# A two-block transformer with graph routing on one core: 128-token groups in the convolution, fill tiles written by ScalarE, gathers placed ahead of loads

## The reference

```
x = x + L1_conv(ln_c(x))        # 3x3 convolution of quantized activations and weights
t = to_tokens(x)                # 50176 tokens of 128 channels
u = ln_t(t)
h = u @ W_gat                   # 4 heads x 4 experts = 16 numbers for each token
a_src, a_dst = (h*att_src).sum(-1), (h*att_dst).sum(-1)       # 4 + 4 numbers
for each destination node: softmax over its edges of leaky_relu(a_src[src] + a_dst[dst]),
    agg = sum of h[src] * alpha                               # 524288 edges and one self loop each
scores = mean over heads of layernorm(agg + b_gat); the top 2 of 4 experts get softmax weights
out = t + sum over experts of weight * (gelu(u @ W1 + b1) @ W2 + b2)
```

## Time and profile before

| | |
|---|---|
| Runs | 10778.33, 10784.39 (median), 10784.59 us |
| The profiled execution | 10787.32 us, span of its instructions 10785.5 us |
| Busy share of the span | POOL 57%, DVE 51%, PE 42%, ACT 36%, PEld 25% |
| Convolution, first to last scatter | 4175.6 to 4800.5 us |
| Graph, first to last gather | 4823.6 to 10024.8 us |
| Combination, first to last gather | 10065.6 to 10707.4 us |
| Granted TensorE clock, mean | 0.732 of full speed |

### The profile page before, as it was taken

One profiled execution on the slowest core, in us unless ns is written; L12 is line 12 of the kernel. 1 busy time (PEld: TensorE's weight loads), 2 busy tenths in 40 slices (PEclk: granted clock), 3 DMA queues, 4 the chain that ended last, 5 costly groups with the idle time before them and its releaser, 6 DMA issues. The chain is left out here.

```text
span 10785.5 us, 111540 instructions
## 1 busy us (share of the span) xinstructions
PE 4563.0 (42%) x31813; PEld 2715.7 (25%) x31813; DVE 5474.9 (51%) x14162; ACT 3929.5 (36%) x9657; POOL 6184.6 (57%) x6259
## 2 busy tenths in 40 slices
PE   0011777777758997873222222223223223223000
PEld 0011555555544444541111111111111101101000
DVE  9987999999986775541121121121121112112487
ACT  0011888888854554332121111112112112112255
POOL 0000555555532224667777777777777777777675
PEclk9755999999978998876666666666666666666555
DMA  0000111111121223543222222222222222222366
GB/s 20 2 0 34 40 39 38 39 41 38 39 78 55 62 62 100 141 121 55 44 46 49 44 46 49 44 42 53 44 42 53 44 42 53 44 42 48 134 250 244
DMA packets 1326096, 663.81 MB, mean 62 GB/s; under 512 B 1058255, under 2 KB 1239100, under 8 KB 1320764
## 3 DMA queue, kind: packets, MB, share of 16 engines
q1 hardware_dynamic: 1142396, 576.49, 19.5%
q0 software_dynamic: 183104, 80.22, 5.7%
HBM read 344.86 MB, written 313.71 MB: 61 GB/s over the span
## 5 line engine op out<-in xcount | busy, mean ns | idle before, releaser
L1832 POOL DMA_INDIRECT gr_rec<-rec,gr_idx x4096 | 3954.2, 965 | 1248.8 <-issue 1248.0
L1853 PE MATMUL gr_p_h<-gr_tT,gr_w 128*128 128x512 f32 x1568 | 849.4, 696 | 3671.7 <-ACT gr_hT L1887 3638.7
L1972 DVE TENSOR_SCALAR gr_pen<-gr_same 128x64 f32<-128x64 f32 x64 | 13.7, 213 | 3170.6 <-DMA gr_rec<-rec,gr_idx 3170.6
L1853 PEld LDWEIGHTS gr_p_h<-gr_tT,gr_w 128*128 128x128 f32 x1568 | 347.6, 227 | 4154.9 <-ACT gr_hT L1887 3723.8
L544 POOL TENSOR_TENSOR at_sq<-at_qk 128x256 f32<-128x256 f32 x392 | 290.2, 740 | 1844.1 <-ACT at_qk L594 1843.9
L1900 ACT ACTIVATE gr_ee<-gr_dd 128x512 f32<-128x512 f32 x64 | 40.3, 629 | 3588.0 <-DVE gr_dd L1991 3588.0
L1858 PE MATMUL gr_p_y<-gr_hT,gr_w 128*128 128x512 f32 x1568 | 688.9, 592 | 0.0
L1952 DVE STREAM_TRANSPOSE gr_z<-gr_yb 128x2048 f32<-128x2048 f32 x98 | 226.5, 2311 | 902.8 <-issue 491.5
L1887 ACT ACTIVATE gr_hT<-gr_p_h,gr_b 128x512 f32<-128x512 f32 x784 | 517.6, 688 | 191.7 <-PE gr_p_h L1853 191.0
L2140 POOL DMA_INDIRECT cb_a<-scan,cb_idx x392 | 499.0, 1273 | 133.7 <-issue 122.4
L1340 POOL DMA_INDIRECT adst<-co_rec,co_idx x448 | 424.5, 948 | 223.3 <-issue 123.1
(11 more groups left out here) (358 smaller groups left out, 13212.1 us busy)
## 6 DMA issues: line engine op xcount, KB each, us to landing
y<-gr_z SPq DMA_DIRECT2D x392, 256.0 KB, 5.4
cb_y<-y SPq DMA_DIRECT2D x28, 3584.0 KB, 13.2
gr_rec<-rec,gr_idx POOLq DMA_INDIRECT x4096, 2.3
scan<-gr_out SPq DMA_DIRECT2D x64, 768.0 KB, 3.8
at_xs<-in_x_win SPq DMA_DIRECT2D x56, 448.0 KB, 3.8
x<-at_x SPq DMA_DIRECT2D x56, 448.0 KB, 4.2
ff_x<-x SPq DMA_DIRECT2D x56, 448.0 KB, 3.4
x<-ff_x SPq DMA_DIRECT2D x784, 32.0 KB
```

The lines of the kernel that those rows point to most:

```text
L1832: nc.gpsimd.indirect_dma_start(out=rec[s][:, j, :], out_offset=None, in_=rec_dram, in_offset=bass.IndirectOffsetOnAxis(ap=idx[s][:, j:j + ...
L1853: nc.tensor.matmul(p_h[m % 4][:, :], w1[:, P * m:P * (m + 1)], tT[b.k][:, :], start=True, stop=True).then_inc(S["hp"], 1)
```

## The change

- Convolution: the tokens of a strip, 8 x 112 = 896, are taken as 7 groups of 128. The matmul for `rec` runs 7 times with 128 tokens, `rec` has 128 partitions x 7 groups, and there are 7 scatters of 128 indices a strip. Their indices are read from columns of `first` directly, so the tile `idx`, its copy on VectorE and its wait are gone. The x3 store has semaphores of its own (`x_out`) and stands ahead of the wait for `rec`; VectorE's x3 waits for that store alone. A strip's node order begins in the middle of a group, so `rec` is stored by four DMAs in place of two.
- Graph: SyncE's first DMA is the index load of chunk 0; GpSimd's first 64 gathers wait for it alone, and the `headr` gather comes after them. VectorE waits for `headr` at chunk 0.
- Combination: the index tile `end` has a semaphore of its own, and its columns are used directly. ScalarE fills both landing tiles at the start, and each later one behind the Exp that makes the inverse deviation (the tile's old content has been read by then).

```diff
-        rec = two("rec", [W, ROWS, REC])
+        rec = two("rec", [P, GROUPS, REC])                        # GROUPS = 7
...
@@ convolve, sync
                     if p.has(-1):
                         s = p.slot(-1)
+                        p.wait("x3", -1, 2)
+                        sp.sem_inc(S["passed"], 1)
+                        dst = x3_dram.rearrange("(y x) c -> x y c", x=W)[:, bass.ds((p.t - 1) * ROWS, ROWS), :]
+                        sp.dma_start(dst, x3[s][:, :, :]).then_inc(S[f"x_out{s}"], 16)
                         p.wait("rec", -1)
                         p.wait("tT", -1, 2)
...
-                        for h in range(2):
-                            dst = rec_dram.rearrange("(y x) c -> x y c", x=W)[:, bass.ds(token_row(nc, p.t - 1, h), HROWS), :]
-                            sp.dma_start(dst, rec[s][:, HROWS * h:HROWS * h + HROWS, :]).then_inc(S[f"out{s}"], 16)
+                        for row, q in ((top, 0), (low + P // 2, full + 1)):
+                            dst = rec_dram[row:row + full * P, :].rearrange("(g p) c -> p g c", p=P)
+                            sp.dma_start(dst, rec[s][:, q:q + full, :]).then_inc(S[f"out{s}"], 16)
+                        for row, lo in ((top + full * P, 0), (low, P // 2)):
+                            sp.dma_start(rec_dram[row:row + P // 2, :], rec[s][lo:lo + P // 2, full, :]).then_inc(S[f"out{s}"], 16)
@@ convolve, tensor
-                        for r in range(ROWS):
-                            mm = nc.tensor.matmul(p_r[:, r, :], tT[s][:, r, :], wcat[:, :], start=True, stop=True)
+                        for q in range(GROUPS):
+                            mm = nc.tensor.matmul(p_r[:, q, :], tokens[:, P * q:P * q + P], wcat[:, :], start=True, stop=True)
@@ convolve, gpsimd
-                        for r in range(ROWS):
-                            nc.gpsimd.indirect_dma_start(out=adst_dram, out_offset=bass.IndirectOffsetOnAxis(ap=idx[s][:, r:r + 1], axis=0),
-                                                         in_=rec[s][:, r, FEAT + GH:REC], in_offset=None, bounds_check=E - 1,
+                        for q in range(GROUPS):
+                            g = (p.t - 1) * GROUPS + q
+                            nc.gpsimd.indirect_dma_start(out=adst_dram, out_offset=bass.IndirectOffsetOnAxis(ap=first[:, g:g + 1], axis=0),
+                                                         in_=rec[s][:, q, FEAT + GH:REC], in_offset=None, bounds_check=E - 1,
@@ convolve, vector
-                        p.wait_lot("out", -2, CONV_OUT)
+                        p.wait_lot("x_out", -2, 16)
...
-                        p.wait_lot("sc", -2, ROWS * 16)
-                        nc.vector.tensor_copy(idx[s][:, :], first[:, bass.ds(p.t * ROWS, ROWS)]).then_inc(S["idx"], 1)
@@ graph_and_experts, sync
+                sp.dma_start(idx[0][:, :], src_dram.rearrange("(p e) -> p e", p=P)[:, 0:CH]).then_inc(S["ix0"], 16)
                 sp.wait_ge(S["set"], 1)
@@ combine, gpsimd
-                pool.wait_ge(S["consts_in"], 48)
-                pool.wait_ge(S["set"], 1)
+                pool.wait_ge(S["end_in"], 16)
...
-                        nc.gpsimd.tensor_copy(a[s][:, :, :], low[:, :, :])
-                        nc.gpsimd.tensor_copy(idx[s][:, :], end[:, bass.ds(p.t * FB, FB)]).then_inc(copied, 1)
-                        pool.wait_ge(copied, p.t + 1)
+                        p.wait("fill", 0)
@@ combine, scalar
+                for i in range(2):
+                    nc.scalar.activation(a[i][:, :, :], low[:, :, :], ACT.Copy).then_inc(S["fill"], 1)
...
                         nc.scalar.activation(rstd[:, :], lnv[:, :], ACT.Exp, scale=-0.5).then_inc(S["act"], 1)
+                        if p.has(3):
+                            nc.scalar.activation(a[p.slot(1)][:, :, :], low[:, :, :], ACT.Copy).then_inc(S["fill"], 1)
```

More of the change, by code:

```diff
@@ L1196 @@
 REC = FEAT + 2 * GH
+GROUPS = WIN * W // P
+FPARTS = 4
+FROWS = B * H * W // P // FPARTS
 def convolve(nc, d, pixels, x2_dram, x3_dram, tT_dram, rec_dram, recs_dram, start_dram, adst_dram):
@@ L1228, in convolve @@
         tT = two("tT", [P, ROWS, W])
-        rec = two("rec", [W, ROWS, REC])
+        rec = two("rec", [P, GROUPS, REC])
         p_c = [ps(f"p_c{i}", [P, HROWS, W]) for i in range(2)]
         p_t = [ps(f"p_t{i}", [P, HROWS, W]) for i in range(2)]
[L1232 to L1237, removed]
+        p_r = ps("p_r", [P, GROUPS, REC])
+        first_i = sb("first_i", [FROWS, FPARTS, P], I32)
+        first_f = sb("first_f", [FROWS, FPARTS, P])
+        first = sb("first", [P, FPARTS * FROWS], I32)
+        p_f = ps("p_f", [P, FPARTS, FROWS])
         p_x = [ps(f"p_x{i}", [W, HROWS, P]) for i in range(2)]
@@ L1240, in convolve @@
         own = {n: ctx.enter_context(nc.semaphore("co_" + n)) for n in (
-            "consts_in", "tanh", "ext", "top", "wq", "x_in0", "x_in1", "out0", "out1", "win", "conv", "xc", "px", "x3", "stat",
-            "rstd", "t", "trp", "tT", "recp", "rec", "first", "firstp", "idx", "passed")}
+            "consts_in", "tanh", "ext", "top", "wq", "x_in0", "x_in1", "x_out0", "x_out1", "out0", "out1", "win", "conv", "xc", "px", "x3", "stat",
+            "rstd", "t", "trp", "tT", "recp", "rec", "first", "firstp", "passed")}
         S = {**own, **dict(zip(("sc0", "sc1"), d["soft"][13:15]))}
@@ L1282, in _ @@
                 pe.wait_ge(S["first"], 1)
-                for b in range(B):
-                    mm = nc.tensor.transpose(p_f[:, b, :], first_f[:, b, :], ident[0:H, 0:H])
+                for b in range(FPARTS):
+                    mm = nc.tensor.transpose(p_f[:, b, :], first_f[:, b, :], ident[0:FROWS, 0:FROWS])
                 mm.then_inc(S["firstp"], 1)
@@ L1391, in _ @@
                 v.wait_ge(S["firstp"], 1)
-                nc.vector.tensor_copy(first[:, :], p_f[:, :, :].rearrange("x b y -> x (b y)")).then_inc(S["first"], 1)
+                nc.vector.tensor_copy(first[:, :], p_f[:, :, :].rearrange("p a g -> p (a g)")).then_inc(S["first"], 1)
                 for k in range(2):
@@ L2076, in combine @@
         S = {n: ctx.enter_context(nc.semaphore("cb_" + n)) for n in (
-            "consts_in", "set", "in0", "in1", "xy0", "xy1", "pre", "f", "sq", "act", "sum", "prod", "out0", "out1", "passed", "passed_sp")}
+            "end_in", "fill", "consts_in", "set", "in0", "in1", "xy0", "xy1", "pre", "f", "sq", "act", "sum", "prod", "out0", "out1", "passed", "passed_sp")}
         S.update(zip(("ga0", "ga1"), d["soft"][11:13]))
@@ L2082, in _ @@
             def _(sp):
-                for dst, src in ((end[:, :], end_dram), (cst[:, :, :], d["g_ln"]), (order[:, :, :, :], d["order"])):
+                sp.dma_start(end[:, :], end_dram).then_inc(S["end_in"], 16)
+                for dst, src in ((cst[:, :, :], d["g_ln"]), (order[:, :, :, :], d["order"])):
                     sp.dma_start(dst, src).then_inc(S["consts_in"], 16)
@@ L2122, in _ @@
             def _(pool):
-                idx = [sb(f"idx{i}", [P, FB], I32) for i in range(2)]
-                copied = ctx.enter_context(nc.semaphore("cb_copied"))
-                pool.wait_ge(S["consts_in"], 48)
-                pool.wait_ge(S["set"], 1)
+                pool.wait_ge(S["end_in"], 16)
                 def emit(p):
```

39 lines of the change are left out of this document (20 added, 19 removed).

## The result

The changed kernel took 10641.76 us (median of 4 runs, 10637.34 to 10645.47) against 10781.72 of the kernel before in the same comparison: a ratio of 0.987, 95% interval 0.9853 to 0.9887, so 140 us less. The forecast was 10640. Its profiled execution took 10637.34, with a span of 10635.6 and a mean granted clock of 0.739.

| Stretch | Before | After | Difference | Forecast |
|---|---|---|---|---|
| start of the span to first scatter | 4175.6 | 4169.7 | -5.9 | 0 |
| first to last scatter's start | 624.9 | 510.7 | -114.2 | -115.3 |
| last scatter's end to the graph's first DMA | 11.0 | 8.2 | -2.8 | +0.2 |
| that DMA to the last gather | 5212.4 | 5203.8 | -8.6 | -7.4 |
| last gather to the combination's first | 40.8 | 39.0 | -1.8 | -2.5 |

A forecast was written before the change was run, and what follows sets the result against it. GpSimd was taken as the bound in all three stages, in the convolution through a ring with VectorE. Gains of 115.3 - 0.2 + 7.4 + 21.5 = 144 us from 10784.39 gave 10640, with 10612 to 10681 holding 8 in 10.

The forecast's parts named there:

- The convolution's ring: Convolution: GpSimd holds VectorE, whose lateness returns to GpSimd; with the waits gone GpSimd sets the pace, stage 115.3 us shorter.
- Rival A: Convolution: TensorE's lower clock keeps every second strip slow, mean 9.5 us a strip, gain 94, total 10662; chance 0.27.
- the two slots: Convolution, argument against Rival A: two slots let GpSimd run through one late strip, leaving TensorE no idle time.
- D: Convolution: TensorE stays at the lower clock throughout, 12.7 to 13.1 us a strip, total 10852, slower; chance 0.04.
- The two small stores: Convolution, SyncE: two more small DMAs a strip, each surely under 0.5 us, costing 0.
- The scatter's price: Convolution: a scatter of 128 indices takes 0.999 us, 1.303 with the gap, so seven take 9.12 a strip.
- The lower end: Convolution: scatters of 128 indices take 0.942 us as with 112, gain 137.5, total 10618; within the forecast's 0.60.
- Rival B: Convolution: VectorE's normalization stops GpSimd, 2.14 us more a strip, 11.26 in all, total 10760; chance 0.03.
- Clears and the graph: Convolution's end: one more semaphore clear, +0.2 us; graph: gathers start 8.7 earlier, `headr` gather costs 1.3, net -7.4.
- The combination: Combination: 13 changes of blocks at 1.46 us each save 19.0, an earlier start 2.5, together 21.5.
- Rival C: Combination: only its start gains, 19.0 us less gain, total 10659; chance 0.06.
- The sum: Whole kernel: 115.3 - 0.2 + 7.4 + 21.5 = 144 us less, median 10640; forecast's chance 0.60.

The follow-up runs named there:

- with the waits alone: Old kernel, convolution still 8 scatters of 112 a strip, but without the index copy, VectorE's scatter wait and x3's wait for `rec` stores: 10727.67 us (0.9944).

## Why the prediction was right

**The convolution's ring.** Right, and shown from both sides: without the waits GpSimd is idle for issue alone, with them it waits for `rec`. Rival A (the clock keeps the ring slow) had 0.27 and falls: the stage's granted clock rose to 0.93, and GpSimd's waits for `rec` come to 4.0 us in 13 scatters, where it was 68.9. That the two slots take up TensorE's late strips, as the prediction argued, fits this but was not tried by itself. D falls with A. The two small stores that a strip has more took SyncE 0.56 us each at the median, not under 0.5, and no row shows that it mattered.

**The scatter's price.** 9.12 us a strip was forecast and 510.7 / 391 x 7 = 9.14 came, by luck: two errors cancel. 0.999 was taken from gathers of the same width; a scatter takes 0.975 on average, 391 x 0.024 = 9.4 us less. The three gaps, which the prediction had at nothing, bring 10.4 us back. The lower end (0.942) was excluded by the number of indices, as the kernel with 112 of 128 shows.

**Rival B, VectorE's normalization stops GpSimd,** falls: 0.97 inside it, and no scatter over 1.2 in the whole stage. The Trainium skill (SBUF — State Buffer, "SBUF: two separate sides") would have GpSimd held for a whole VectorE instruction in a 2-port mode or with two SBUF inputs. This trace agrees for the additions of two tiles, in either form, and for the graph: held beside the product of two tiles, not beside the transpose of one. L1450 neither bears it out nor speaks against it. Apart from two columns of scalars it reads one tile, but no row shows whether it ran in a 2-port mode, and its eight instructions take 0.27 us each, as short as those that left most gathers of the combination at 1.00.

**Clears and the graph.** +0.2 was forecast for the convolution's end and -2.8 came. What was left out is that the time from the last scatter's end to the graph's first DMA changes: it is 2.8 shorter with seven groups of 128 than with eight rows of 112, and 4.7 in all with seven of 112 indices. Why was not tried. The load at the head of SyncE's queue gave 8.6 at the start, as forecast (8.7), again by two errors that cancel: it landed after 1.69 instead of 2.2, and from the landing to the gather 0.86 passed instead of 0.2. The 1.3 charged for `headr` do not show. From first to last gather it took 5201.2 in both, although one more stands between them now; the others were 0.3 ns shorter on average, which over 4096 is as much.

**The combination.** 17.6 of 19.0, and 1.8 of 2.5. At the start it was not the fill that was missed but the 0.90 us from the landing of the index load to the first gather, where nothing was charged. Between the blocks the 19.0 came, 0.30 stands where 1.76 stood; the gaps before gathers 114, 226 and 338 grew by 4.5 us in all (to 3.65, 3.94 and 3.92), and the gathers were 2.8 shorter in sum. Both are small against the spread: the changed combination took 617 to 627 in the executions where nothing but the convolution or the gathers' bytes differed, the old one 633 to 643. Rival C (only the start gains) falls with that.

**The sum.** 144 forecast, 140 measured by the medians. The mechanism was right in each stage. That the number fits to 4 us is in part luck, by the errors above.

## What to carry to other kernels

Where an engine that writes descriptors is the bound, count indices per instruction and instructions, and take away whatever lets its lateness come back to it through another engine's buffer; here the two were worth 50 and 66 us. When that engine runs without a pause, look at what stretches its instructions: VectorE's long two-tile operations cost 65 us of a stage of 624. Cutting them into seven gave 48 back, and then VectorE set the pace; cutting them into fourteen gave that up again. After each such step ask anew which engine waits for which. Price an indirect DMA from a row with the same number of indices, the same direction and the same bounds check, and look through that row's idle times for gaps.

## What was not expected of the hardware

- An indirect DMA's time on GpSimd goes by its indices, not by its bytes: 0.942 with 112 and 0.972 with 128 in the scatters; 0.997 in the gathers with 16 bytes an index, 0.999 with 96.
- There is a gap of 1 to 9 us on GpSimd, put down to nothing but issue, at every 112th indirect DMA of 128 indices and every 126th of 112, in the convolution and the combination but not in the graph, and not in 448 scatters of 112. It was longest (8.8) where the DMA engines were busiest (75%). Its cause is open.
- The mean granted clock of the convolution does not follow TensorE's busy share: 0.80 at 79% before, 0.90 at 77% with the waits alone, 0.93 at 82% after. What decides is open.
- A VectorE addition and a multiply-and-add of 1792 elements from two SBUF tiles both take 2.02 us, and both stretch gathers from 1.0 up to 2.8. A transpose of 2048 elements from one tile, 2.31 us, stretches none.
- GpSimd began its first indirect DMA of a stage 0.86 to 0.91 us after the load that it waited for had landed, in the graph and in the combination.
